# One-core attention stack: half of the first batch's query and key projections moved behind the first attention, its first stack loaded during it

## The chip, the cores and the metric

The kernel runs on 1 core of one Trainium2 chip. The metric is the device time of one launch in microseconds (us), as the median of several runs; lower is better. TensorE's matmul side is called PE, VectorE DVE, ScalarE ACT, GpSimd POOL, SyncE SP. SP issues nearly all DMAs.

## The reference

Two batches of 1024 tokens, width 256, 16 heads of 16, all in float32:

```
x  = x + attention(x Wq, ctx Wk, ctx Wv)      # a0: 77 context rows as keys
n  = layernorm(x)                             # norm 1
x  = x + attention(n Wq', n Wk', n Wv') Wo'   # a1: 1024 keys per batch
n  = layernorm(x)
x  = x + attention(n Wcq, ctx Wck, ctx Wcv) Wco   # a2: 77 keys again
x  = x + gelu(layernorm(x) W1) W2
```

## The kernel before

**Names.** Tokens stand in four blocks (tb 0 to 3) of 512; blocks 0 and 1 are the first batch. The attentions are A0, A1 and A2. Heads go in groups of four: 8 groups (g), and for each two halves of 512 queries, so 16 "q" per attention. An attention is a loop of steps t: 16 for A0 and A2 (one per q), 128 for A1 (eight tiles of 128 keys per q). A step makes four score matmuls (L815), whose exponentials ACT takes (L949), and the value products of the step before (L831).

**Row maxima.** A softmax row needs its maximum first. A "max" unit is a score matmul into the banks SM (PE L763 for A0 and A2, L758 for A1) and a reduction of it by DVE (L1065, L1062). A1's unit is 1.2 us of DVE; 26 of them ("lead") and one "rows" entry run ahead of A1's first step, the others two per step. "rows" turns a q's maxima into rows (PE L774 or L771, DVE copy L1075 or L1074 into mrow) that SP sends into the queries' tile (L636, L632); the scores of q wait for it. In A0 the rows of q + 2 are made in step q; in A1 those of q + 1 in key tile 4 of q.

**Stacks.** A group's queries and keys stand in a stack in SBUF. They get there by way of DRAM: a projection (L700, one chunk is half of the width for one block: 2 matmuls of 512 columns, 4 in the trace's count) is split into two parts, by ACT (L888) and DVE (L990); SP stores them to q_rows or k_rows (L554, two DMAs of 256 KB per chunk), and the function `stack` loads a group: for A1 10 DMAs (L584, L591), 1.5 MB, after SP itself has waited until the chunks that it reads have landed. Chunk i = 0 of the first batch feeds groups 0 and 1, chunk i = 1 groups 2 and 3. A1 has three stack buffers; buffer 0 and the keys' half of buffer 1 are free during A0. Padding rows of the buffers are set by POOL (`pad`, L1187); a stack load waits until they are.

**The order.** Nothing schedules itself: each engine walks the same lists and does its own part of each entry, strictly in order. UNDER_A0, UNDER_A1 and UNDER_A2 say what is put into which step; BEFORE_A1 is the list between A0 and A1. ("side", A1, a, b) is entries a to b of A1's 27 units ahead ("max" 0 to 19, "rows" 0, "max" 20 to 25). "x1" adds A0's result to a block and takes its statistics (DVE L1039, L1027, L1030; POOL takes the root), "norm" scales it (L1047), "t_ln1" transposes it (L704; ACT L920 or DVE L1002 write it to fm), "vals_s" is the value projection (L710, read by DVE L1007). "proj_kc" is the key projection of A2's context (two chunks of 154 columns), needed only by A2. A PE, DVE or SP entry that waits holds all that stands behind it on that engine.

**When stacks are loaded in A1.** The method `stacks_at` gives the step: 16 (g - 2) for group g, unless a projection that stands in UNDER_A1 in the first half pushes it back:

```
            for w in self.products(k):
                for g in range(QUAD + 2 * w[2], QUAD + 2 * w[2] + 2) if w[0][:5] == "proj_" else []:
                    at[g] = max(at[g], k + self.lag[1])
```

Of the kernel before, what the change touches and what calls it, by code (L numbers as in the profile page):

```python
# [35 lines left out]
KC = DIM // P  # L36
NT = TOK // P
BLK = 512
NB = TOK // BLK
TPB = BLK // P  # L40
QUAD = 4
# [6 lines left out]
SROWS = len(BANDS) * HD  # L48
# [22 lines left out]
def block_of(stage, tb, first=0, count=None):  # L71
    return [(stage, tb, i) for i in range(first, first + (count or PER[stage]))]


def chunks(i, *stages, tb):

    return [(stage, tb, i) for stage in stages]


def one_in_two(first, work):  # L80
# [5 lines left out]


UNDER_A0 = {
    **{n: [("load", n), ("pads", "a1", n)] for n in range(NB)},
    8: [("load", 4), ("load", 5)],  # L90
    9: [("x1", 0)],
    10: [("norm", 0, 0), ("x1", 1), ("load", 6), ("load", 7)],
    11: [("norm", 0, 1)] + block_of("t_ln1", 0),
    12: block_of("proj_q1", 0) + block_of("t_ln1", 1),
    13: block_of("proj_k1", 0),
    14: block_of("proj_q1", 1),
    15: block_of("proj_k1", 1),
}
UNDER_A1 = {
    **one_in_two(67, block_of("t_a1", 0) + block_of("out_1", 0) + [("stats", 1, 0)]  # L100
                 + block_of("t_a1", 1) + [("norm", 1, 0)] + block_of("out_1", 1) + [("stats", 1, 1)]
                 + block_of("t_ln2", 0) + [("norm", 1, 1)] + chunks(0, "proj_q2", tb=0) + block_of("t_ln2", 1)
                 + chunks(0, "proj_q2", tb=1) + chunks(1, "proj_q2", tb=0) + chunks(1, "proj_q2", tb=1)),
    98: [("pads", "a2", 0), ("keys", "a2")],
    112: [("pads", "a2", 1)],
    114: [("values", "a2", 0)],
# [30 lines left out]
class Attention:  # L137
# [61 lines left out]
    def chores(self, t):  # L199
# [3 lines left out]
A0 = Attention(0, 1, CTX, lead=12, rows_ahead=2, rows_at=0, buffers=4, banks=4, under=UNDER_A0,  # L203
               split_by=("pool", "dve"), lag=(0, 1))
A1 = Attention(1, SEQ // P, P, lead=26, rows_ahead=1, rows_at=4, buffers=3, banks=2, under=UNDER_A1,
               split_by=("pool", "pool"), lag=(1, 2))
# [11 lines left out]
BEFORE_A0 = [("proj_k0", 0), ("proj_q0", 0), ("keys", "a0"), ("proj_q0", 1), ("stack", "a0", 0), ("vals_c", 0),  # L218
             ("values", "a0", 0), ("stack", "a0", 1), ("proj_q0", 2), ("stack", "a0", 2), ("proj_q0", 3),
             ("side", A0, 0, len(A0.before)), ("stack", "a0", 3)]  # L220
BEFORE_A1 = [("stack", "a1", 0), ("vals_s", 0), ("x1", 2), ("vals_s", 1), ("x1", 3),
             ("norm", 0, 2), ("side", A1, 0, 2), ("t_ln1", 2),
             ("norm", 0, 3), ("side", A1, 2, 4), ("t_ln1", 3), ("pads", "a1", NB)]
SPREAD = [(stage, tb, i, 1) for stage, tb in (("proj_q1", 2), ("proj_k1", 2), ("proj_q1", 3), ("proj_k1", 3))
          for i in range(KC)]
BEFORE_A1 += [w for i, chunk in enumerate(SPREAD) for w in (("side", A1, 2 * i + 4, 2 * i + 6), chunk)]
BEFORE_A1 += [("values", "a1", 0), ("proj_kc", 0), ("side", A1, 2 * len(SPREAD) + 4, len(A1.before)), ("stack", "a1", 1),
              ("vals_s", 2), ("vals_s", 3), ("stack", "a1", 2)]
BEFORE_A2 = []
AFTER_A2 = [("t_a2", 2), ("t_a2", 3), ("up", 0), ("out_2", 2), ("out_2", 3), ("norm", 2, 2), ("norm", 2, 3),  # L230
# [1 line left out]
            ("down", 2), ("down", 3)]  # L232
PLAN = [(BEFORE_A0, A0), (BEFORE_A1, A1), (BEFORE_A2, A2), (AFTER_A2, None)]

# [13 lines left out]
def xattn_kernel(nc, xT_d, x_d, cT_d, ident_d, cols_d, rows_d, wq0, wk0, wv0, sa_w, so_w,  # L248
# [8 lines left out]
    with ctx:  # L257
# [21 lines left out]
        Kst = [stacks[:, n, 0] for n in range(A1.buffers)]  # L279
        Qst = [stacks[:, n, 1] for n in range(A1.buffers)]  # L280
# [108 lines left out]
        st_done = sem("st_done")  # L389
# [778 lines left out]
        def _(pool):  # L1168
# [4 lines left out]
            def step(ins):  # L1173

                ins.then_inc(pool_step, 1)
                steps[0] += 1
                pool.wait_ge(pool_step, steps[0])

            def space():

                used[0] += 1
                return gp.memset(spacer[:, used[0]:used[0] + 1], 0.0)


            def pad(tile, first, value):

                step(gp.memset(tile[first:first + 32].bitcast(FP32), value))  # L1187

            def padded():

                step(space())
                space().then_inc(pad_ready, 1)
                step(space())
# [8 lines left out]
            step(gp.memset(prob[64:P, :, :, :], 0.0))  # L1202
            step(gp.memset(nexp[:, :], -0.5))
            padded()

            def stationary(att, g):

# [24 lines left out]
            def pads(att, part):  # L1232

                step(space())
                if att is A1:
                    if part < 2:
                        pad(Kst[part], 32, 1.0)
                        pad(Kst[part], SROWS, 1.0)
                    elif part == 2:
                        pad(Qst[0], 32, 0.0)  # L1240
                        pad(Qst[0], SROWS, 0.0)
                        padded()
                    elif part == NB:
                        pool.wait_ge(st_done, A0.steps * QUAD)
                        pad(Qst[1], 32, 0.0)
                        pad(Qst[2], 32, 0.0)
                        pad(Kst[2], 32, 1.0)
                        pad(Kst[2], SROWS, 1.0)
                        padded()
                    step(space())  # L1250
                    return
                pool.wait_ge(st_done, (att.t0 - (2 - part) * HALVES * A1.kt) * QUAD)
                if part == 0:
                    pad(Kst[2], SROWS, TWO_ONES)
                    pad(Qst[2], SROWS, 0.0)
                elif part == 1:
                    pad(Qst[0], SROWS, 0.0)
                    pad(Kst[0], SROWS, 0.0)
                else:
                    pad(Qst[1], SROWS, 0.0)  # L1260
                padded()
# [145 lines left out]
```

## Time and profile before

| what | us |
|---|---|
| median of 3 runs (803.64 to 807.79) | 805.66 |
| the profiled execution's own time | 805.98 |
| its span in the trace | 804.2 |
| PE busy | 727.4 (90%) |
| DVE busy | 533.0 (66%) |
| ACT busy | 441.2 (55%) |
| POOL busy | 154.4 (19%) |
| chain that ended last: PE, DVE, DMA | 58%, 21%, 10% |

Times below are counted from the start of the span. A0's steps run from 48.85 to about 131, the list BEFORE_A1 from there to 200.86, A1 from 200.86.

### The profile page before, as it was taken

The numbers are of one execution on the slowest core, as the hardware profiler recorded it, in microseconds if no ns is written. First come the engines' busy times: TensorE is split into PE (matmuls) and PEld (weight loads), VectorE is DVE, ScalarE is ACT, GpSimd is POOL, SyncE is SP. The second block draws the span as 40 slices with busy tenths as digits, with TensorE's granted clock in tenths as the row PEclk, the third lists the DMA queues.
The fourth block names the chain that finished last, engine by engine and source line by source line (L and its number), as shares of the span: only waits on it lengthen the run. The fifth ranks groups of instructions, "written<-read, shape, count | busy, mean of one in ns | idle before, by whom it ended". The sixth has DMA issues, their size and how long they took to land.

```text
span 804.2 us, 13587 instructions
## 1 busy us (share of the span) xinstructions
PE 727.4 (90%) x5200; PEld 358.1 (45%) x5200; DVE 533.0 (66%) x851; ACT 441.2 (55%) x802; POOL 154.4 (19%) x341
## 2 busy tenths in 40 slices
PE   7568899488999999999999999997988997999998
PEld 3334445335333333333433433333454564556767
DVE  3436864697999999999899898852477774230001
ACT  4435544121888888887677677665635644323120
POOL 7335240431000000000001013150143223030000
PEclk9869899699999999999999999998999999999999
DMA  7977714536705050505013010016355600000001
GB/s 264 180 173 144 160 46 175 72 124 156 104 2 82 2 82 3 82 2 81 2 26 59 1 26 2 21 46 94 61 137 125 107 3 1 1 7 20 26 14 39
DMA packets 39087, 55.35 MB, mean 69 GB/s; under 512 B 8944, under 2 KB 24048, under 8 KB 39024
## 3 DMA queue, kind: packets, MB, share of 16 engines
q1 hardware_dynamic: 38736, 54.42, 32.3%
q8 instruction: 41, 0.67, 0.4%
q14 instruction: 22, 0.18, 0.1%
q10 hardware_dynamic: 288, 0.08, 0.1%
HBM read 36.31 MB, written 17.25 MB: 67 GB/s over the span
## 4 chain that ended last, share of the span: by engine, by line
PE 58%; DVE 21%; DMA 10%; ACT 3%; SPq 3%; issue 3%; POOL 1%; DVEq 0%; POOLq 0%; ACTq 0%
DVE nm L1062 15%; PE PV L831 14%; PE ST L815 11%; PE ST L723 5%; PE ST L719 5%; PE SM L758 5%; PE SM L710 3%; DMA V<-mrow 3%; DMA stacks<-mrow 3%; PE SM L700 3%; PE PV L723 2%; PE PV L719 2%; PE SM L704 2%; PE SM L763 2%; PE ST L710 2%
## 5 line engine op out<-in xcount | busy, mean ns | idle before, releaser
L949 ACT ACTIVATE prob<-ST 128x512 f32<-128x512 f32 (+1 forms) x640 | 349.6, 596 | 168.0 <-PE ST L815 158.9
L1062 DVE TENSOR_REDUCE nm<-SM 128x2 f32<-128x1024 f32 x256 | 308.8, 1221 | 16.1 <-PE SM L758 14.5
L831 PE MATMUL PV<-prob,Vst 128*32 128x256 f32 (+1 forms) x2304 | 202.9, 425 | 5.4 <-ACT pvT L938 2.8
L815 PE MATMUL ST<-stacks 64*128 64x512 f32 (+1 forms) x608 | 171.2, 483 | 6.5 <-DMA stacks<-mrow 4.1
L758 PE MATMUL SM<-stacks 64*128 64x512 f32 x512 | 109.5, 424 | 19.2 <-DMA stacks<-k_rows 10.2
L815 PEld LDWEIGHTS ST<-stacks 64*128 64x128 f32 (+1 forms) x608 | 61.8, 173 | 140.9 <-ACT prob L949 102.5
L1065 DVE TENSOR_REDUCE nm<-SM 128x4 f32<-128x308 f32 x128 | 58.0, 472 | 52.5 <-PE SM L763 50.8
L831 PEld LDWEIGHTS PV<-prob,Vst 128*32 128x32 f32 x2304 | 46.3, 109 | 95.4 <-issue 68.1
L758 PEld LDWEIGHTS SM<-stacks 64*128 64x128 f32 x512 | 49.5, 188 | 40.9 <-DVE nm L1062 22.8
L1017 DVE TENSOR_TENSOR X<-ST,X 128x256 f32<-128x256 f32 x18 | 7.5, 422 | 90.5 <-PE ST L723 73.7
L938 ACT ACTIVATE pvT<-PV 128x512 f32<-128x512 f32 x48 | 28.7, 599 | 33.7 <-PE PV L831 33.6
L719 PE MATMUL ST<-fm,V 128*128 128x512 f32 x96 | 42.6, 593 | 0.3 <-ACT fm L920 0.3
L1277 POOL CAST mp<-na 128x16 fp32r<-128x16 f32 x16 | 3.2, 198 | 199.8 <-DVE na L1097 199.8
L1303 POOL TENSOR_TENSOR X<-X,bc 128x256 f32<-128x256 f32 x48 | 34.2, 743 | 26.7 <-DVE A L1047 26.7
L763 PE MATMUL SM<-stacks 96*128 96x77 bf16 x384 | 30.9, 208 | 6.9 <-DMA stacks<-q_parts 4.1
L763 PEld LDWEIGHTS SM<-stacks 96*128 96x128 bf16 x384 | 26.6, 106 | 23.1 <-issue 9.0
L780 PE MATMUL SM<-ident,pvT 128*128 128x128 f32 x192 | 31.0, 285 | 2.8 <-ACT pvT L938 1.2
L1187 POOL MEMSET stacks<- 32x2048 f32 x18 | 32.4, 1800 | 1.0
L700 PE MATMUL SM<-fm,early 128*128 128x512 f32 x64 | 31.0, 607 | 0.0
L719 PEld LDWEIGHTS ST<-fm,V 128*128 128x128 f32 x96 | 18.1, 190 | 21.7 <-issue 20.8
L700 PE MATMUL ST<-fm,early 128*128 128x512 f32 x48 | 25.1, 654 | 1.9 <-DMA fm<-in_xT 1.0
L927 ACT ACTIVATE early<-ST,cols 128x512 f32<-128x512 f32 x12 | 8.3, 688 | 33.1 <-PE ST L719 33.1
(114 smaller groups left out, 718.3 us busy)
## 6 DMA issues: line engine op xcount, KB each, us to landing
stacks<-q_parts SPq DMA_DIRECT2D x72, 128.0 KB, 4.9
q_parts<-split SPq DMA_DIRECT2D x16, 384.0 KB
q_rows<-parts SPq DMA_DIRECT2D x16, 256.0 KB
k_rows<-parts SPq DMA_DIRECT2D x16, 256.0 KB
stacks<-q_rows SPq DMA_DIRECT2D x16, 256.0 KB
stacks<-k_rows SPq DMA_DIRECT2D x16, 256.0 KB
V<-q_parts SPq DMA_DIRECT2D x24, 128.0 KB, 5.3
fm<-in_xT SPq DMA_DIRECT2D x4, 512.0 KB, 7.5
```

The costliest lines, as they stand in the source:

```text
L700: last = mm(ps[:, 0:width], weight[:, k, w0 + i * P:w0 + (i + 1) * P], src[:, k, c0:c0 + width], start=(k == 0), stop=(k == KC - 1))
L710: last = mm(ps[:, 0:DIM], fm[:, k, t0:t0 + P], weight[:, k, w0:w0 + DIM], start=(k == 0), stop=(k == KC - 1))
L719: last = mm(ps[:, 0:BLK], w_1[:, k, i * P:(i + 1) * P], fm[:, k, tb * BLK:(tb + 1) * BLK], start=(k == 0), stop=(k == KC - 1))
L723: last = mm(ps[:, 0:DIM], hid[tb % 2][:, f, i * P:(i + 1) * P], w_2[:, f, :], start=(f == 0), stop=(f == FF // P - 1))
L758: last = mm(ps[:, s * BLK:(s + 1) * BLK], Q[rows, n, c0:c0 + P], Kst[g % att.buffers][rows, n, c * BLK:(c + 1) * BLK], start=True, stop=True)
L763: last = mm(ps[:, h * CTX:(h + 1) * CTX], Q[0:SROWS, h, c0:c0 + P], keys_of(att, g, h, 0)[0:SROWS], start=True, stop=True)
L815: mm(ST[0:att.keys, n % 3, :], keys_of(att, g, h, kt), QST[att.name][g % att.buffers][rows, at, j * BLK:(j + 1) * BLK], start=True, stop=T ...
L831: last = mm(PV[h * 32:(h + 1) * 32, queries], Vst[:, g % 2, kt, h, :], prob[:, t % 2, h, queries], start=(kt == 0 and first == 0), stop=(k ...
L949: act_fn(prob[0:att.keys, t % 2, h, :], ST[0:att.keys, n % 3, :], ACT.Exp, scale=SCALE if att.whole else 1.0).then_inc(exp_done, 1)
L1062: ins = vec.tensor_reduce(nm2[:, q % 2, c, tile, 2 * n:2 * n + 2], ps.rearrange("p (s k) -> p s k", s=2), AX.X, ALU.max, negate=True)
L1065: ins = vec.tensor_reduce(nm[:, q % 2, v, :], ps[:, 0:QUAD * CTX].rearrange("p (h k) -> p h k", h=QUAD), AX.X, ALU.max, negate=True)
L1303: ins = gp.tensor_tensor(X[:, t, :], X[:, t, :], bc[:, (B_SO, B_CO, B_F2)[n], :], ALU.add)
```

## The change

In UNDER_A0 the four chunks i = 1 of proj_q1 and proj_k1 of blocks 0 and 1 leave steps 12 to 15; the four chunks i = 0 stand in steps 12 and 13, and the load of stack 0 stands in step 13. The moved chunks stand in BEFORE_A1. There the load of stack 1 comes first, after the one round of padding that is left; the two first max units stand ahead of both "x1"; and proj_kc has gone to steps 40 and 42 of A1. The padding of buffer 0 and of the keys of buffer 1 moves from A0's first steps to POOL's start.

```diff
--- before.py
+++ after.py
@@ -86,21 +86,20 @@
 
 
 UNDER_A0 = {
-    **{n: [("load", n), ("pads", "a1", n)] for n in range(NB)},
+    **{n: [("load", n)] for n in range(NB)},
     8: [("load", 4), ("load", 5)],
     9: [("x1", 0)],
     10: [("norm", 0, 0), ("x1", 1), ("load", 6), ("load", 7)],
     11: [("norm", 0, 1)] + block_of("t_ln1", 0),
-    12: block_of("proj_q1", 0) + block_of("t_ln1", 1),
-    13: block_of("proj_k1", 0),
-    14: block_of("proj_q1", 1),
-    15: block_of("proj_k1", 1),
+    12: chunks(0, "proj_q1", "proj_k1", tb=0) + block_of("t_ln1", 1),
+    13: chunks(0, "proj_q1", "proj_k1", tb=1) + [("stack", "a1", 0)],
 }
 UNDER_A1 = {
     **one_in_two(67, block_of("t_a1", 0) + block_of("out_1", 0) + [("stats", 1, 0)]
                  + block_of("t_a1", 1) + [("norm", 1, 0)] + block_of("out_1", 1) + [("stats", 1, 1)]
                  + block_of("t_ln2", 0) + [("norm", 1, 1)] + chunks(0, "proj_q2", tb=0) + block_of("t_ln2", 1)
                  + chunks(0, "proj_q2", tb=1) + chunks(1, "proj_q2", tb=0) + chunks(1, "proj_q2", tb=1)),
+    **{40 + 2 * i: [("proj_kc", 0, i)] for i in range(KC)},
     98: [("pads", "a2", 0), ("keys", "a2")],
     112: [("pads", "a2", 1)],
     114: [("values", "a2", 0)],
@@ -218,13 +217,13 @@
 BEFORE_A0 = [("proj_k0", 0), ("proj_q0", 0), ("keys", "a0"), ("proj_q0", 1), ("stack", "a0", 0), ("vals_c", 0),
              ("values", "a0", 0), ("stack", "a0", 1), ("proj_q0", 2), ("stack", "a0", 2), ("proj_q0", 3),
              ("side", A0, 0, len(A0.before)), ("stack", "a0", 3)]
-BEFORE_A1 = [("stack", "a1", 0), ("vals_s", 0), ("x1", 2), ("vals_s", 1), ("x1", 3),
-             ("norm", 0, 2), ("side", A1, 0, 2), ("t_ln1", 2),
-             ("norm", 0, 3), ("side", A1, 2, 4), ("t_ln1", 3), ("pads", "a1", NB)]
+BEFORE_A1 = [("pads", "a1", 0), ("stack", "a1", 1), ("proj_q1", 0, 1, 1), ("proj_k1", 0, 1, 1), ("vals_s", 0),
+             ("side", A1, 0, 2), ("x1", 2), ("proj_q1", 1, 1, 1), ("proj_k1", 1, 1, 1), ("vals_s", 1), ("x1", 3),
+             ("norm", 0, 2), ("side", A1, 2, 4), ("t_ln1", 2), ("norm", 0, 3), ("side", A1, 4, 6), ("t_ln1", 3)]
 SPREAD = [(stage, tb, i, 1) for stage, tb in (("proj_q1", 2), ("proj_k1", 2), ("proj_q1", 3), ("proj_k1", 3))
           for i in range(KC)]
-BEFORE_A1 += [w for i, chunk in enumerate(SPREAD) for w in (("side", A1, 2 * i + 4, 2 * i + 6), chunk)]
-BEFORE_A1 += [("values", "a1", 0), ("proj_kc", 0), ("side", A1, 2 * len(SPREAD) + 4, len(A1.before)), ("stack", "a1", 1),
+BEFORE_A1 += [w for i, chunk in enumerate(SPREAD) for w in (("side", A1, 2 * i + 6, 2 * i + 8), chunk)]
+BEFORE_A1 += [("values", "a1", 0), ("side", A1, 2 * len(SPREAD) + 6, len(A1.before)),
               ("vals_s", 2), ("vals_s", 3), ("stack", "a1", 2)]
 BEFORE_A2 = []
 AFTER_A2 = [("t_a2", 2), ("t_a2", 3), ("up", 0), ("out_2", 2), ("out_2", 3), ("norm", 2, 2), ("norm", 2, 3),
@@ -1202,6 +1201,10 @@
             step(gp.memset(prob[64:P, :, :, :], 0.0))
             step(gp.memset(nexp[:, :], -0.5))
             padded()
+            for tile, value in ((Kst[0], 1.0), (Qst[0], 0.0), (Kst[1], 1.0)):
+                pad(tile, 32, value)
+                pad(tile, SROWS, value)
+            padded()
 
             def stationary(att, g):
 
@@ -1233,21 +1236,12 @@
 
                 step(space())
                 if att is A1:
-                    if part < 2:
-                        pad(Kst[part], 32, 1.0)
-                        pad(Kst[part], SROWS, 1.0)
-                    elif part == 2:
-                        pad(Qst[0], 32, 0.0)
-                        pad(Qst[0], SROWS, 0.0)
-                        padded()
-                    elif part == NB:
-                        pool.wait_ge(st_done, A0.steps * QUAD)
-                        pad(Qst[1], 32, 0.0)
-                        pad(Qst[2], 32, 0.0)
-                        pad(Kst[2], 32, 1.0)
-                        pad(Kst[2], SROWS, 1.0)
-                        padded()
-                    step(space())
+                    pool.wait_ge(st_done, A0.steps * QUAD)
+                    pad(Qst[1], 32, 0.0)
+                    pad(Qst[2], 32, 0.0)
+                    pad(Kst[2], 32, 1.0)
+                    pad(Kst[2], SROWS, 1.0)
+                    padded()
                     return
                 pool.wait_ge(st_done, (att.t0 - (2 - part) * HALVES * A1.kt) * QUAD)
                 if part == 0:
```

PE between A0's last transposes (L780, L779 in the changed kernel; all lines below 101 stand one lower there) and the first projection of block 2. Before:

```order
L780 MATMUL SM<-ident,pvT 128x128 x8
L710 MATMUL ST<-early,fm 128x256 x2
L710 MATMUL PV<-early,fm 128x256 x2
L710 MATMUL ST<-early,fm 128x256 x6
L710 MATMUL PV<-early,fm 128x256 x2
L710 MATMUL ST<-early,fm 128x256 x4
L758 MATMUL SM<-stacks 128x512 x4
L704 MATMUL ST<-ident,A 128x128 x4
L704 MATMUL PV<-ident,A 128x128 x4
L758 MATMUL SM<-stacks 128x512 x4
L704 MATMUL ST<-ident,A 128x128 x8
L758 MATMUL SM<-stacks 128x512 x4
```

After the change:

```order
L779 MATMUL SM<-ident,pvT 128x128 x8
L699 MATMUL ST<-fm,early 128x512 x2
L699 MATMUL PV<-fm,early 128x512 x2
L709 MATMUL ST<-early,fm 128x256 x6
L709 MATMUL PV<-early,fm 128x256 x2
L757 MATMUL SM<-stacks 128x512 x4
L699 MATMUL ST<-fm,early 128x512 x4
L709 MATMUL ST<-early,fm 128x256 x2
L709 MATMUL PV<-early,fm 128x256 x2
L709 MATMUL ST<-early,fm 128x256 x4
L757 MATMUL SM<-stacks 128x512 x4
L703 MATMUL ST<-ident,A 128x128 x4
```

The two moved chunks of block 0 stand where the second half of the value projections stood, the first two max units (SM<-stacks) stand behind four value projections, and two more chunks and four value projections stand behind them.

DVE from the first "x1" of that list to the max units (TENSOR_REDUCE). Before:

```order
L1039 TENSOR_TENSOR X<-X,A 128x256 x4
L1027 BN_STATS stats<-X 128x6 x4
L1030 BN_AGGR mv<-stats 128x2 x4
L1007 TENSOR_TENSOR V<-ST,bc 128x4x64
L1007 TENSOR_TENSOR V<-PV,bc 128x4x64
L1007 TENSOR_TENSOR V<-ST,bc 128x4x64 x2
L1039 TENSOR_TENSOR X<-X,A 128x256 x4
L1027 BN_STATS stats<-X 128x6 x4
L1030 BN_AGGR mv<-stats 128x2 x4
L1047 TENSOR_SCALAR A<-X,mv,rstd 128x256 x4
L1062 TENSOR_REDUCE nm<-SM 128x2 x2
L1047 TENSOR_SCALAR A<-X,mv,rstd 128x256 x4
```

After the change:

```order
L1061 TENSOR_REDUCE nm<-SM 128x2 x2
L1038 TENSOR_TENSOR X<-X,A 128x256 x4
L1026 BN_STATS stats<-X 128x6 x4
L1029 BN_AGGR mv<-stats 128x2 x4
L989 SCALAR_TENSOR_TENSOR parts<-ST,cols,parts 128x512 x2
L1006 TENSOR_TENSOR V<-ST,bc 128x4x64
L1006 TENSOR_TENSOR V<-PV,bc 128x4x64
L1006 TENSOR_TENSOR V<-ST,bc 128x4x64 x2
L1038 TENSOR_TENSOR X<-X,A 128x256 x4
L1026 BN_STATS stats<-X 128x6 x4
L1029 BN_AGGR mv<-stats 128x2 x4
L1046 TENSOR_SCALAR A<-X,mv,rstd 128x256 x4
```

Both "x1" (X<-X,A and the two rows behind it) and the first "norm" (A<-X,mv,rstd) stood ahead of the first max units and now stand behind them, with two readings of moved chunks (parts<-ST).

SP in A1, around the load of stack 4 (zeros, q_rows, k_rows; c_parts is proj_kc's store, mrow the rows). Before:

```order
L632 DMA stacks<-mrow 2x4x128 x8
L584 DMA stacks<-zeros 2x16x128
L591 DMA stacks<-q_rows 32x2x1024
L591 DMA stacks<-q_rows 16x2x1024
L591 DMA stacks<-k_rows 32x2x1024
L591 DMA stacks<-k_rows 16x2x1024
L584 DMA stacks<-zeros 2x16x128
L591 DMA stacks<-q_rows 32x2x1024
L591 DMA stacks<-q_rows 16x2x1024
L591 DMA stacks<-k_rows 32x2x1024
L591 DMA stacks<-k_rows 16x2x1024
L632 DMA stacks<-mrow 2x4x128 x8
```

After the change:

```order
L562 DMA c_parts<-split 128x3x154
L583 DMA stacks<-zeros 2x16x128
L590 DMA stacks<-q_rows 32x2x1024
L590 DMA stacks<-q_rows 16x2x1024
L590 DMA stacks<-k_rows 32x2x1024
L590 DMA stacks<-k_rows 16x2x1024
L583 DMA stacks<-zeros 2x16x128
L590 DMA stacks<-q_rows 32x2x1024
L590 DMA stacks<-q_rows 16x2x1024
L590 DMA stacks<-k_rows 32x2x1024
L590 DMA stacks<-k_rows 16x2x1024
L631 DMA stacks<-mrow 2x4x128 x4
```

The load of stack 4 stood at step 32, two sets of rows (8 DMAs) ahead of it and the rows of q = 5 and 6 behind it; now it stands at step 42, behind proj_kc's first store and right ahead of the rows of q = 6.

## Rows read from the trace of the kernel before

**Rows 1.** The chain that ended last, 125 to 156: start us, us, what

```profile
131.79 6.36 DMA k_rows<-parts
...
143.03 9.30 DMA stacks<-k_rows
...
152.47 0.81 PE SM L758 x2
```

**Rows 2.** Timeline of PE: start, us, line, operation, in brackets idle before and its releaser

```profile
113.59 1.88 PE L700 MATMUL SM<-fm,early 128*128 128x512 f32 x4
...
152.47 1.22 PE L758 MATMUL SM<-stacks 64*128 64x512 f32 x4 [10.17 <-DMA stacks<-k_rows]
...
200.86 0.50 PE L815 MATMUL ST<-stacks 64*128 64x512 f32 x2 [0.78 <-DVE V L1007]
```

**Rows 3.** Timeline of SP's queue: first store of step 12, stack 0, stack 4

```profile
113.49 3.37 SPq L554 DMA_DIRECT2D q_rows<-parts  x4
...
138.17 0.73 SPq L584 DMA_DIRECT2D stacks<-zeros  x1
...
283.91 0.64 SPq L584 DMA_DIRECT2D stacks<-zeros  x1
```

**Rows 4.** Windows: from:to, length, PE clock, DMA share, GB/s

```profile
116.00:121.50 5.50, 1.00 0.50 172
...
285.40:295.40 10.00, 1.00 1.01 159
```

**Rows 5.** Timeline of DVE

```profile
114.36 0.80 DVE L1002 TENSOR_SCALAR fm<-SM,cols 128x512 f32<-128x512 f32 x1
...
120.42 0.40 DVE L1075 COPY mrow<-SM 12x512 bf16<-12x512 bf16 x1
...
139.22 1.42 DVE L1039 TENSOR_TENSOR X<-X,A 128x256 f32<-128x256 f32 x4
...
142.16 0.39 DVE L1007 TENSOR_TENSOR V<-ST,bc 128x256 f32<-128x256 f32 x1
...
146.39 1.34 DVE L1047 TENSOR_SCALAR A<-X,mv,rstd 128x256 f32<-128x256 f32 x4
153.37 2.36 DVE L1062 TENSOR_REDUCE nm<-SM 128x2 f32<-128x1024 f32 x2 [5.64 <-PE SM L758]
...
159.87 2.36 DVE L1062 TENSOR_REDUCE nm<-SM 128x2 f32<-128x1024 f32 x2 [0.59 <-PE SM L758]
...
186.14 6.86 DVE L1062 TENSOR_REDUCE nm<-SM 128x2 f32<-128x1024 f32 x6
```

**Rows 6.** Timeline of POOL: A0's start, and the padding ahead of A1

```profile
23.50 0.24 POOL L1229 COPY Vst<-Vc 77x64 f32<-77x64 f32 x1 [6.73 <-DVE Vc L1012]
30.21 2.39 POOL L1310 TENSOR_TENSOR parts<-parts,split 128x512 f32<-128x512 f32 x2 [6.47 <-ACT split L882]
...
159.97 7.36 POOL L1187 MEMSET stacks<- 32x2048 f32 x4
```

**Rows 7.** Timeline of PE in A0's steps 3 and 5

```profile
64.53 0.38 PE L774 MATMUL SM<-identb,mp 128*12 128x128 bf16 x4 [1.71 <-POOL mp L1289]
...
71.87 0.41 PE L815 MATMUL ST<-stacks 128*77 128x512 bf16 x1 [0.62 <-DMA stacks<-mrow]
```

**Rows 8.** The chain that ended last, the row DMA of A0's step 3

```profile
65.45 6.37 DMA stacks<-mrow
```

**Rows 9.** Windows: PE, PEld, DVE, ACT, POOL busy (instructions), PE clock, DMA share, GB/s

```profile
152.40:160.00 7.60, 7.11 (x28) 4.79 (x28) 6.04 (x9) 3.11 (x4) 2.85 (x6) 0.50 0.00 0
```

**Rows 10.** Timeline of PE: proj_kc's second chunk, then A1's steps 42, 44 and 48

```profile
184.81 0.69 PE L700 MATMUL PV<-ctxT,early 128*128 128x154 f32 x4
...
311.63 0.50 PE L815 MATMUL ST<-stacks 64*128 64x512 f32 x2
...
318.25 0.28 PE L771 MATMUL SM<-ident,mp 128*32 128x128 f32 x1
...
327.06 0.50 PE L815 MATMUL ST<-stacks 64*128 64x512 f32 x2
```

## The prediction

> **What bounds the kernel now.** I read the chain of waits in order of time first, since the change touches one place, the passage from A0 to A1. There the chain leaves the engines: a store of a key part takes 6.36 us, then SP issues stack 0, whose last DMA takes 9.30 us, and PE starts the first max unit at 152.47 [rows 1]. The timeline of PE shows the price: 10.17 us idle [rows 2]. That is what the change is after. But the stretch behind it, up to A1's first step at 200.86, must be read as well, and there the timeline of DVE decides: two max units and one reading of a chunk follow each other almost without a gap from 159.87 until the last six units end at 193.00 (186.14 + 6.86) [rows 5]. So behind the stack DVE is the bound. And what does DVE do while PE waits for the stack? It adds x1 of two blocks and scales one (139.22 to 147.73) [rows 5]. PE's idle time is not the kernel's idle time.
>
> **When stack 0 arrives after the change.** (a) A0's start. POOL's six memsets of 1.84 us (7.36 / 4) [rows 6], 11.0 us, move from A0's first steps to POOL's start. There POOL is idle 6.73 and 6.47 us, 13.2 in all, around a 0.24 us copy that nothing wants before A0's steps [rows 6]: hidden; without that cover they would push the split of block 3's queries back. What they free is 1.71 us of PE in step 3 [rows 7]. Little of it survives: step 5 waits for its row until 71.87 [rows 7], a small DMA issued at 65.45 that takes 6.37 us [rows 8], because the six loads of a stack stand in front of it. Only the issue of those moves up, by about half a microsecond. I take 0.8 us; the bounds are 0 and 3.4 (twice the 1.71, since the step behind the stall is slowed as well).
>
> (b) Step 13's first chunk is now of block 1, whose fm is written by DVE until 115.16 (114.36 + 0.80) [rows 5], where the old one started at 113.59 [rows 2]: +1.6 us. The row copy of that step, before at 120.42 to 120.82 [rows 5], ends at 120.8 + 1.6 - 0.8 = 121.6. SP issues the row in 0.8 us and then the stores of both chunks, from 122.4.
>
> (c) Four stores took from 113.49 [rows 3] to 121.5, where their data ends [rows 4]: 8.0 us. So they land at 130.6 with 0.2 for the notice, where SP got on at 138.17 before [rows 3] with 14 of 16 stores done: six fewer.
>
> (d) Ten DMAs of a stack took from 283.91 [rows 3] to 295.4 [rows 4] when nothing was in their way: 11.5 us. Before it was 14.3 (138.17 to 152.47), with chunk stores still moving. I take 11.5 and 0.3 for the start: **the first max unit at 142.4 instead of 152.47, 10.1 us earlier** (bounds 141 and 145). PE, relieved of two chunks on balance, waits there still, some 4 us.
>
> **What stands behind it.** Call D the start of DVE's first max unit, 0.9 us after PE's: 153.37 before [rows 5], 143.3 after. Before, the last unit ended at D + 39.6. After the change DVE has, in its order: two units 2.3 (to D + 2.3); x1 of block 2, 2.9 (139.22 to 142.16 [rows 5]), D + 5.2; two readings of moved chunks 0.7 each, D + 6.5; four readings of values, the last held by PE, D + 7.9; x1 of block 3, D + 10.8; norm 1.3, D + 12.2; two units, D + 14.5; norm, D + 15.8; two units, D + 18.1; then the row of chunks, which began at D + 6.5 (159.87) before and kept 33.1 us. It has one unit fewer behind its chunks (the two that stand earlier, less the one that the last chunk's row entry displaces): 31.8. The last unit ends at D + 50.1. So **10.5 us of work moved from under the wait to behind it**: two x1 5.9, one norm 1.3, two chunk readings 1.4, value readings 1.4, the rest order. The 10.1 us are eaten by it. From the last unit to A1's first step it stays 7.9 us (193.0 to 200.86).
>
> **PE's clock.** After the wait of 10 us PE ran at 0.50 of its clock, which is 1.2 GHz, for 7.60 us, with 7.11 us busy, and DVE only 6.04 [rows 9]. Before there was little for PE to do there. Now two chunks of 1.9 us and four value projections of 0.9 stand there, 7.3 us at full speed, which is about what DVE takes (7.9). If the clock is at half for the first 4 us, PE is 2 us late, and with it both x1. I take 2.0 less 0.4 for the transposes, which now run at full clock: +1.6 (bounds 0 and 5). The Trainium skill (TensorE: Matmul & The Clock Gate, "What's actually happening") states that the throttled state is the default and sustained activity releases it. By that rule the new wait of 4 us, too, may cost the clock; if it doesn't, the sum is that of the rival "clock kept".
>
> **proj_kc and stack 4.** In BEFORE_A1 the two chunks were covered by DVE. In A1's steps PE and DVE are both full. A chunk of four 154-column matmuls keeps PE 0.55 to 0.69 us [rows 10], with 0.3 us of DVE; I take 1.2 us for both (bounds 0.5 and 2). And stack 4 goes from step 32 to step 42. Its use as keys and queries is late enough (the first max unit of group 4 is in step 51). But the rows of q = 6 are queued right behind it on SP. Step 42 starts at 311.63 [rows 10]; with ACT's and POOL's parts of proj_kc and the store, SP starts the stack near 316.6 (the step's 2.5 us, 0.6 for the first chunk, and some 1.9 for ACT, POOL and the store), and by the 11.5 us above its data ends at 328.1. The row DMAs, ready at about 319, behind step 44's transposition at 318.25 [rows 10], come in behind that data as in rows 8, at 328.5. Step 48 wants them at 327.06 [rows 10] + 1.2 = 328.3. I take +0.4 (bounds 0 and 3). Next late, if that fails, is nothing: stack 5 loads at step 48 as before.
>
> **Sum.** -10.1 + 10.5 + 1.6 + 1.2 + 0.4 = +3.6 us on the profiled execution's 805.98, so 809.6; that execution stands 0.3 above the median 805.66, so **809.3** as a median. POOL's second round of padding (7.4 us from A0's last score) and the load of stack 1 lie beside waits; the chunk stores queued behind stack 1 land by about 160 (142.1 + 11.5 + the 8.0 of four stores, less the overlap), and the chunks of block 2 want those buffers from D + 21.6, 165, on; past that point each us late would cost one.
>
> **The rivals.** *Padding stalls fully given back* (not slower): if step 5's row is not held by the loads, A0 gains 3.4 instead of 0.8 and the stack chain with it: 809.3 - 2.6 = 806.7. For it: the 1.71 us are real PE idle time. Against: rows 8. It decides from an A0 gain of about 3 us on; one of 4.4 would make the change's sum zero.
> *Clock kept*: 809.3 - 2.0 = 807.3. For it: the wait is 4 us instead of 10.
> *Work hides after all*: DVE had 1.6 us free of 7.60 in rows 9. If the moved work uses these, 1.6 less: 807.7. Against: the order is fixed, and the gaps are waits for PE at its half clock.
> *Stacks in each other's way* (slower): stack 1 is issued from 136 on, while stack 0's data moves until 142. If the engines share out their time, stack 0 lands up to 4 us later: 813.3. Against: in rows 8 a later DMA waits behind the earlier ones. The Trainium skill (DMA: Bandwidth & Descriptors, "Queues, rings and completion order") says the same, that each engine takes its ring's descriptors in order; by it this rival costs nothing and 809.3 stands.
>
> **How the numbers follow.** Forecast 0.45, own range 807 to 812; padding 0.15; clock 0.13; work hides 0.07; stacks 0.12; gains together 0.08 (all three 803.1). About 0.5%, 4.0 us, is what a measurement of this kernel can tell from no change. Slower by more starts at 809.7: nearly half of the forecast and the rival of the stacks, and large clock or row costs, 0.42. Faster by more (under 801.6) needs all three gains and an overrated term besides: 0.07. Between: 0.51. Range 802.5 to 814: it takes in all single rivals and leaves out a sum below them.
>
> **What would show it.** In the changed kernel's trace: PE's wait for k_rows ends near 142.4 and is 3 to 6 us long; SP starts stack 0 near 130.6; DVE's first "x1" of block 2 stands behind two max units; A1's first step is at 202 to 204 instead of 200.86; PE's clock is at half for some 4 us behind the wait; a wait of PE for mrow at step 48 of under 2 us; A1's steps 40 to 43 are 0.6 us longer each for a chunk. The prediction is wrong if A0's step 5 starts more than 2 us earlier, or if the time between the first max unit and A1's first step is not near 60 us (48.4 before).

## The result and the profile after

The changed kernel takes **821.37 us** (median of 4 runs, 817.22 to 823.72), the kernel before 806.01 beside it (median of 4, 803.64 to 807.79): a ratio of 1.019, 95% interval 1.0155 to 1.0224. It is slower, by four times what was forecast. The profiled execution took 820.4 us, with a span of 818.6, which is 14.4 more than before.

I divided both spans, and later those of all experiments, at the same four events: A0's first step, SP's issue of stack 0, PE's first max unit (the stack has landed), A1's first step.

| us | A0's first step | to issue of stack 0 | to first max unit | to A1's first step | to the end | span |
|---|---|---|---|---|---|---|
| before | 48.85 | 89.3 | 14.3 | 48.4 | 603.3 | 804.2 |
| after | 50.10 | 82.5 | 14.6 | 61.3 | 610.1 | 818.6 |
| difference | +1.3 | -6.8 | +0.3 | +12.9 | +6.8 | +14.4 |

A0's first step lay between 46.1 and 50.1 in the kernels of this study. Kernels that are alike up to there differ in it by up to 4.0 us (50.1 in the changed kernel, 46.1 in x1_first below), so the first column can't be put down to the change.

The chain that ended last, in order of time, answers to [rows 1]:

```profile
126.20 6.38 DMA k_rows<-parts
...
137.45 9.59 DMA stacks<-k_rows
...
147.18 1.22 PE SM L757 x4
```

PE's timeline at the same places as [rows 2], with the first wait behind the stack, and step 48 of A1:

```profile
116.02 1.96 PE L699 MATMUL SM<-fm,early 128*128 128x512 f32 x4 [1.55 <-DVE fm L1001]
...
147.18 1.22 PE L757 MATMUL SM<-stacks 64*128 64x512 f32 x4 [8.82 <-DMA stacks<-k_rows]
148.33 4.82 PE L699 MATMUL ST<-fm,early 128*128 128x512 f32 x8
...
161.41 1.08 PE L703 MATMUL ST<-ident,A 128*128 128x128 f32 x4 [4.15 <-DVE A L1046]
...
208.49 0.50 PE L814 MATMUL ST<-stacks 64*128 64x512 f32 x2 [0.78 <-DVE V L1006]
...
341.87 0.79 PE L814 MATMUL ST<-stacks 64*128 64x512 f32 x2 [5.33 <-DMA stacks<-mrow]
```

Three things stand there. The wait for the stack is hardly shorter (8.82 us instead of 10.17), though it ends 5.3 us earlier. A new wait of 4.15 us follows, for a norm that was done long before in the old order. And there is a wait of 5.33 us for a q's rows at step 48, where there was none [rows 10]. SP's timeline gives the issues that belong to them (compare [rows 3]):

```profile
124.15 1.21 SPq L553 DMA_DIRECT2D q_rows<-parts  x2
...
132.63 0.73 SPq L583 DMA_DIRECT2D stacks<-zeros  x1
...
138.00 0.65 SPq L583 DMA_DIRECT2D stacks<-zeros  x1
...
326.22 0.67 SPq L583 DMA_DIRECT2D stacks<-zeros  x1
...
331.38 2.62 SPq L631 DMA_DIRECT2D stacks<-mrow  x4
```

And DVE's timeline behind the stack, beside [rows 5]:

```profile
148.08 2.36 DVE L1061 TENSOR_REDUCE nm<-SM 128x2 f32<-128x1024 f32 x2 [9.26 <-PE SM L757]
150.35 1.42 DVE L1038 TENSOR_TENSOR X<-X,A 128x256 f32<-128x256 f32 x4
...
156.98 1.42 DVE L1038 TENSOR_TENSOR X<-X,A 128x256 f32<-128x256 f32 x4
...
159.91 1.35 DVE L1046 TENSOR_SCALAR A<-X,mv,rstd 128x256 f32<-128x256 f32 x4
...
195.06 5.74 DVE L1061 TENSOR_REDUCE nm<-SM 128x2 f32<-128x1024 f32 x5
```

DVE is idle for 9.26 us and then does both x1 and the norm, which it did under the wait before. Windows sum it up. Their columns are the window, its length, busy us of PE, PEld (PE's weight loads), DVE, ACT and POOL (instructions), PE's clock as a share of 2.4 GHz, the DMA share and GB/s. First the stretch from the first max unit to A1's first step in the kernel before:

```profile
152.47:200.86 48.39, 42.10 (x142) 22.41 (x143) 40.38 (x48) 10.45 (x18) 13.75 (x21) 0.88 0.44 116
```

The same in the changed kernel, then pieces of it and two windows behind the wait at step 48:

```profile
147.18:208.49 61.31, 49.69 (x158) 26.30 (x159) 50.79 (x82) 9.99 (x14) 9.84 (x16) 0.86 0.57 141
143.00:150.00 7.00, 2.82 (x6) 1.37 (x7) 1.92 (x2) 0.00 (x0) 0.00 (x0) 0.50 1.07 139
...
161.00:169.00 8.00, 6.71 (x25) 4.78 (x26) 7.41 (x10) 3.12 (x4) 6.22 (x9) 0.50 0.34 133
...
198.50:201.00 2.50, 2.41 (x6) 1.71 (x7) 2.30 (x3) 0.00 (x0) 0.00 (x0) 0.50 0.65 168
...
342.00:344.00 2.00, 2.00 (x12) 0.56 (x12) 0.87 (x1) 1.08 (x2) 0.00 (x0) 0.50 1.07 122
344.00:346.00 2.00, 2.00 (x18) 0.91 (x16) 1.06 (x2) 1.14 (x3) 0.09 (x1) 0.71 1.06 170
```

DVE has 10.4 us more work in this stretch (50.79 less 40.38), PE 7.6 more. PE's clock is at half, 1.2 GHz, in four places, each behind a time in which PE had waited or had little to do.

### The profile page after: what moved, and what is told of

Read it like the earlier page. It is cut to its first block, busy times and chain, and to the rows that moved or that the text cites. A ratio compares the mean times of both kernels' runs of the same rounds, so it can differ in the third digit from the quotient of the medians.

```text
span 818.6 us, 13576 instructions
## 1 busy us (share of the span) xinstructions
PE 729.7 (89%) x5200; PEld 358.6 (44%) x5200; DVE 533.4 (65%) x853; ACT 440.5 (54%) x800; POOL 154.0 (19%) x332
## 4 chain that ended last, share of the span: by engine, by line
PE 60%; DVE 21%; DMA 10%; SPq 3%; ACT 3%; issue 3%; POOL 1%; DVEq 0%; POOLq 0%; ACTq 0%
PE PV L830 14%; DVE nm L1061 13%; PE ST L814 11%; PE ST L722 5%; PE ST L718 5%; PE SM L757 5%; PE SM L709 3%; PE SM L699 2%; DMA stacks<-mrow 2%; PE ST L699 2%; DMA V<-mrow 2%; PE ST L709 2%; PE SM L762 2%; PE SM L703 2%; PE PV L722 2%
## 5 line engine op out<-in xcount | busy, mean ns | idle before, releaser
L699 PE MATMUL ST<-fm,early 128*128 128x512 f32 x60 | 32.9, 684 | 2.2 <-DMA fm<-in_xT 1.3
L1186 POOL MEMSET stacks<- 32x2048 f32 x18 | 32.4, 1799 | 10.4 <-PE ST L814 9.5
L779 PE MATMUL SM<-ident,pvT 128*128 128x128 f32 x192 | 30.5, 281 | 2.8 <-ACT pvT L937 1.2
L1277 POOL CAST mp<-nm 128x16 bf16<-128x16 f32 x32 | 6.3, 197 | 110.9 <-DVE nm L1064 110.8
L703 PE MATMUL SM<-ident,A 128*128 128x128 f32 x112 | 20.0, 309 | 7.0 <-DVE A L1046 6.1
```

Source lines behind the costliest of these rows:

```text
L699: last = mm(ps[:, 0:width], weight[:, k, w0 + i * P:w0 + (i + 1) * P], src[:, k, c0:c0 + width], start=(k == 0), stop=(k == KC - 1))
L703: last = nc.tensor.transpose(ps[:, n * P:(n + 1) * P], A[:, tb * TPB + n, i * P:(i + 1) * P], ident[:, :])
```

## The experiments

Two losses had to be told apart: the passage behind the stack (+12.9) and A1 (+6.8). For each I had a theory, and in the passage two rivals: that the stacks delay each other, and that PE's clock, not DVE's order, is the price. Parts of the span are read from one traced execution of each kernel; medians are of all its runs. `...` in a code cut stands for code left out.

### The A1 side: proj_kc, and what it does to stack 4

The first kernel, kc_back, is the changed one with proj_kc back in the list ahead of A1:

```diff
-    **{40 + 2 * i: [("proj_kc", 0, i)] for i in range(KC)},
-BEFORE_A1 += [("values", "a1", 0), ("side", ...
+BEFORE_A1 += [("values", "a1", 0), ("proj_kc", 0), ("side", ...
```

> The changed kernel with the two chunks of proj_kc put back into the list ahead of A1, so that stack 4 is loaded at step 32 again. Theory (late stack): PE's wait of 5.3 us for the rows at step 48 comes from stack 4's load standing right ahead of those rows; it goes, and with it the two chunks' own 1.3 us and half a microsecond of half clock: 814.5 instead of 821.4, and no wait of PE for mrow over 1 us in A1 between steps 40 and 50. Rival (passage only): the whole loss is made ahead of A1's first step and the wait is one that another place would show instead: 820 to 821.

Measured: 811.10 us (10 runs, 807.18 to 815.86), ratio to before 1.0076, 1.0041 to 1.0111. That is 3.4 us less than the theory said. The part from A1's first step to the end is 603.5 us, as before (603.3), and there is no wait for rows at step 48. The traced execution also had PE's clock at 0.94 in the passage, the highest of all kernels here.

The second, kc_no_push, leaves proj_kc in A1, but it no longer pushes stack 4 back:

```diff
-    ... if w[0][:5] == "proj_" else []:
+    ... if w[0][:5] == "proj_" and w[0] != "proj_kc" else []:
```

> The changed kernel with proj_kc still in A1's steps 40 and 42, but the rule that pushes a stack's load behind a projection doesn't count it, so stack 4 loads at step 32. Theory (late stack): the 5.3 us wait goes, the chunks' own cost stays: 815.5, about 1.3 above the kernel with proj_kc put back. Rival (the chunks themselves, in steps where PE and DVE are full, with their readings on ACT and POOL): 819 to 821, since the load's place alone does nothing.

Measured: 813.52 us (4 runs, 811.96 to 815.59), ratio 1.0114, 1.0064 to 1.0163. The part from A1's first step on is 603.1 us: the two chunks in A1's steps cost nothing that can be seen there. The medians can't exclude the 1.2 us that were forecast for them: this one is 2.4 us above that of kc_back, and the intervals of the two ratios overlap. In SP's timeline of this kernel stack 4 leaves at 291.84, and the rows of q = 6 have no load right ahead of them:

```profile
291.84 0.65 SPq L583 DMA_DIRECT2D stacks<-zeros  x1
...
328.59 2.60 SPq L631 DMA_DIRECT2D stacks<-mrow  x4
```

The third, kc_alone, is the kernel before with only this part of the change, the push with it:

```diff
+    **{40 + 2 * i: [("proj_kc", 0, i)] for i in range(KC)},
-BEFORE_A1 += [("values", "a1", 0), ("proj_kc", 0), ("side", ...
+BEFORE_A1 += [("values", "a1", 0), ("side", ...
```

> The kernel before with one part of the change alone: proj_kc in A1's steps 40 and 42, with the load of stack 4 pushed to step 42. Theory (late stack): a wait for the rows of about 5 us at step 48 appears here as well, 1.3 us for the chunks: 806.0 + 6.8 = 812.8. Rival (the wait needs what the rest of the change does to A1): 807.3.

Measured: 813.25 us (4 runs, 810.27 to 814.77), ratio 1.0104, 1.0053 to 1.0155. PE's timeline shows the same wait at step 48:

```profile
333.36 0.80 PE L816 MATMUL ST<-stacks 64*128 64x512 f32 x2 [6.24 <-DMA stacks<-mrow]
```

So the push is the cause, not the chunks: with it the wait is there, without it the wait is gone. A1's part is 6.8 us longer in the changed kernel and 6.0 in kc_alone. Of the 6.8, 5.33 are the wait; behind it PE ran at half its clock for some 3.2 us (all of 342 to 344, and 58% of the next window, whose clock is 0.71), which is 1.6 us. By the medians the push is 7.9 us (821.37 less 813.52), and the push with the chunks 7.0 (813.25 less 806.26, the kernel before beside kc_alone).

### The padding alone

The kernel before with only the padding moved to POOL's start (shown are the lines added and the first that goes; the old padding code goes as in the change):

```diff
-    **{n: [("load", n), ("pads", "a1", n)] for n in range(NB)},
+    **{n: [("load", n)] for n in range(NB)},
+            for tile, value in ((Kst[0], 1.0), (Qst[0], 0.0), (Kst[1], 1.0)):
+                pad(tile, 32, value)
+                pad(tile, SROWS, value)
+            padded()
```

> The kernel before with the padding of buffer 0 and of the keys of buffer 1 at POOL's start, nothing else. Theory (A0 held by its row DMAs, as predicted): step 5 waits longer for its row instead of step 3 for POOL, 0 to 1 us faster, 805 to 806. Rival (padding stalls given back): 802.6. Rival (POOL's memsets at the start slow what runs beside them): A0's first step later by about 1.2 us as in the changed kernel, 807.

Measured: 804.96 us (10 runs), ratio 1.0005, 0.9977 to 1.0034. From A0's first step to the issue of stack 0 it takes 89.3 us, exactly as before. PE's wait of 1.71 us in step 3 is gone, and the wait for the row DMA of step 5 is longer, 3.61 us instead of 0.62:

```profile
66.97 0.62 PE L815 MATMUL ST<-stacks 128*77 128x512 bf16 x1 [3.61 <-DMA stacks<-mrow]
```

But that wait doesn't take all: step 5's row releases PE 20.8 us behind A0's first step (66.97 less 46.21), against 23.0 before (71.87 less 48.85). These 2.3 us are lost in the steps behind it. Step 9's first score is 0.6 us ahead (83.75 less 46.21, against 86.98 less 48.85), and the value products at 106.25 stand where those at 108.85 stood, 60.0 us behind A0's first step. What takes them there was not isolated: the chain of before passes through a further row DMA (90.87), that of pads_alone through x1 and the norm on DVE. The rival "padding stalls fully given back" is gone.

### The passage: do the stacks delay each other?

This kernel, stack1_late, is kc_back with stack 1 issued behind the moved chunks' stores, so that stack 0 has the queue for itself:

```diff
-BEFORE_A1 = [("pads", "a1", 0), ("stack", "a1", 1), ("proj_q1", 0, 1, 1), ...
+BEFORE_A1 = [("pads", "a1", 0), ("proj_q1", 0, 1, 1), ...
-             ... ("proj_k1", 1, 1, 1), ("vals_s", 1), ("x1", 3),
+             ... ("proj_k1", 1, 1, 1), ("stack", "a1", 1), ("vals_s", 1), ("x1", 3),
```

> Stands on the kernel with proj_kc put back (811.1). One edit: stack 1 is issued behind the stores of all moved chunks instead of right behind stack 0. Theory (stacks in each other's way): stack 0 takes 11.5 us from its first issue instead of 14.4, PE's first max unit comes 2.9 us earlier, and so does A1's first step: 808.2. Rival (a stack takes 14 to 15 us at this place whatever stands behind it, as it did in the kernel before and in all runs so far): 811.

Measured: 813.33 us (9 runs, 806.32 to 815.84), ratio 1.0100, 1.0069 to 1.0130. Stack 0 takes 13.6 us from issue to first max unit, against 14.4 in kc_back. The 0.8 us lie within what stack 0 takes in all twelve kernels, the kernel before included (13.6 to 15.0), and the median did not fall. A stack takes about 14 us here, whether a second one stands behind it or not.

### The passage: the order of DVE's work

x1_first is kc_back with both x1 and the first norm ahead of the first two max units, but the moved chunks of block 1 still behind them:

```diff
-             ("side", A1, 0, 2), ("x1", 2), ("proj_q1", 1, 1, 1), ("proj_k1", 1, 1, 1), ("vals_s", 1), ("x1", 3),
-             ("norm", 0, 2), ("side", A1, 2, 4), ...
+             ("x1", 2), ("x1", 3), ("norm", 0, 2), ("side", A1, 0, 2), ("proj_q1", 1, 1, 1), ("proj_k1", 1, 1, 1),
+             ("vals_s", 1), ("side", A1, 2, 4), ...
```

> Stands on the kernel with proj_kc put back (811.1). One edit: both x1 and the first norm stand ahead of the first two max units in the list, so DVE does them while stack 0 is loaded. Theory (cover lost): 7.2 us of DVE work leaves the stretch behind the stack, PE's wait of 4.1 us for the norm goes, and from the first max unit to A1's first step it is 51 to 52 us instead of 58.4: 804. Rival (PE's half clock and its two moved chunks set the stretch): 809 to 811.

Measured: 809.24 us (10 runs, 805.06 to 814.60), ratio 1.0059, 1.0028 to 1.0089. DVE's busy time in the passage fell from 50.61 (kc_back) to 43.52 us, and the stretch did not follow: 58.0 us after 58.4 (by the medians it gained 1.9). The timelines of PE and DVE show why; the window of the stretch stands below them:

```profile
143.65 1.22 PE L756 MATMUL SM<-stacks 64*128 64x512 f32 x4 [8.90 <-DMA stacks<-k_rows]
144.80 5.44 PE L698 MATMUL ST<-fm,early 128*128 128x512 f32 x8
...
160.87 3.78 PE L698 MATMUL ST<-fm,early 128*128 128x512 f32 x4
```

```profile
149.35 0.75 DVE L988 SCALAR_TENSOR_TENSOR parts<-ST,cols,parts 128x512 fp32r<-128x512 f32 x1 [2.45 <-ACT parts L886]
...
165.47 0.75 DVE L988 SCALAR_TENSOR_TENSOR parts<-ST,cols,parts 128x512 fp32r<-128x512 f32 x1 [3.01 <-ACT parts L886]
```

```profile
143.65:201.65 58.00, 51.02 (x165) 26.51 (x166) 43.52 (x54) 11.68 (x20) 7.83 (x15) 0.87 0.59 150
```

PE is busy 51.02 us of 58.00. The chunks behind the max unit run at half clock (a pair takes 5.44 us, and a chunk at 160.87 3.78 instead of 1.98), and DVE, which reads them behind ACT, waits 2.45 and 3.01 us for them. So my theory, that DVE's order alone makes the stretch long, falls: with that work gone, PE with its own moved work, partly at half clock, is the bound. How much of the missing gain is the moved work and how much the clock was not isolated: the mean clock was 0.87 here and 0.94 in kc_back, an estimate of 4 us of PE's time (13% of 58.0 less 6% of 58.4). Both edits together, combo:

> Both edits together on the kernel with proj_kc put back: x1 and norm ahead of the first max units, stack 1 behind the moved chunks' stores. Theory (cover lost, and stacks in each other's way): 801 to 802, faster than the kernel before (806.3). Rival (a stack's time doesn't depend on the one behind it): 804.

Measured: 808.96 us (6 runs), ratio 1.0035, 1.0002 to 1.0067; stretch 57.8 us. Both the theory (801 to 802) and its rival (804) were too low, since both took x1_first's gain for given. The edits don't add to anything that can be seen over x1_first alone.

The counter-test, x1_late, is the kernel before with only the first two max units drawn ahead of both x1 and the first norm. They come to stand ahead of block 1's value projections (`vals_s` 1) too:

```diff
-BEFORE_A1 = [("stack", "a1", 0), ("vals_s", 0), ("x1", 2), ("vals_s", 1), ("x1", 3),
-             ("norm", 0, 2), ("side", A1, 0, 2), ("t_ln1", 2),
+BEFORE_A1 = [("stack", "a1", 0), ("vals_s", 0), ("side", A1, 0, 2), ("x1", 2), ("vals_s", 1), ("x1", 3),
+             ("norm", 0, 2), ("t_ln1", 2),
```

> The kernel before with one edit: its first two max units stand ahead of both x1 and the first norm, so that this DVE work no longer lies under PE's wait for stack 0. Theory (cover lost): first max unit at the same time, A1's first step later by the 7.2 us of that work less the gaps that DVE has behind it: 811 to 813. Rival (the moved chunks are what costs, not this work): 806 to 807.

Measured: 814.76 us (4 runs, 813.92 to 819.36), ratio 1.0138, 1.0099 to 1.0177: about 10 us, more than expected. PE's timeline:

```profile
149.70 1.22 PE L758 MATMUL SM<-stacks 64*128 64x512 f32 x4 [12.76 <-DMA stacks<-k_rows]
...
161.54 1.09 PE L704 MATMUL ST<-ident,A 128*128 128x128 f32 x4 [5.09 <-DVE A L1047]
```

With no projection moved out of A0, the stretch grows from 48.4 to 58.7 us, as in kc_back, and the wait for the norm is there. Taking the cover from under the wait is by itself enough for what the whole change does to the passage. The cover taken away is not DVE's alone, though: four value projections of PE, with their four readings on DVE, left it along with both x1 and the norm, which the expectation had overlooked, and PE's wait for the stack is 12.76 us instead of 10.17. DVE's share and PE's are not told apart by this kernel.

### Filling the wait with everything that there is

If both engines' moved work is the price, both must go back under the wait. fill_wait is kc_back once more, with all four moved chunks, both blocks' values, both x1 and the first norm ahead of the first max unit:

```diff
-BEFORE_A1 = [..., ("proj_k1", 0, 1, 1), ("vals_s", 0),
-             ("side", A1, 0, 2), ("x1", 2), ("proj_q1", 1, 1, 1), ("proj_k1", 1, 1, 1), ("vals_s", 1), ("x1", 3),
-             ("norm", 0, 2), ("side", A1, 2, 4), ...
+BEFORE_A1 = [..., ("proj_k1", 0, 1, 1), ("proj_q1", 1, 1, 1), ("proj_k1", 1, 1, 1), ("vals_s", 0),
+             ("x1", 2), ("vals_s", 1), ("x1", 3),
+             ("norm", 0, 2), ("side", A1, 0, 2), ("side", A1, 2, 4), ...
```

> The change with proj_kc back in BEFORE_A1, and with everything that PE and DVE can do while stack 0 is on its way put ahead of the first two max units: the four moved chunks, the value projections of blocks 0 and 1, both x1 and the first norm. PE then has some 13 us of work from 129 on, DVE some 12. Theory (the stretch grew because the work that had covered the wait stood behind it, and the rest was PE at half its clock after an idle wait): PE's wait for k_rows falls from 8.6 to 9.4 us to under 2.5, the clock stays at full behind it, and the time from the first max unit to A1's first step falls from 58 to 48 to 51 us; A1 starts near 194 to 197 with A0's start at 48, and the time is 797 to 803 us, under before. Rival (the moved work keeps the same length wherever it stands, since PE or DVE are full over the whole passage and the stack's arrival doesn't decide): the first max unit is late by the work that stands ahead of it, the sum of both is as in x1_first, and the time is 807 to 811.

Measured: **801.43 us** (8 runs, 799.71 to 804.46), before 805.73 beside it (19 runs): ratio 0.9949, 0.9927 to 0.9971. It is faster than before, and 20 us faster than the change. PE's wait:

```profile
146.25 1.22 PE L756 MATMUL SM<-stacks 64*128 64x512 f32 x4 [2.50 <-DMA stacks<-k_rows]
```

DVE's first reduction:

```profile
149.10 4.61 DVE L1060 TENSOR_REDUCE nm<-SM 128x2 f32<-128x1024 f32 x4
```

The windows ahead of the max unit and behind it:

```profile
131.00:146.25 15.25, 12.75 (x48) 8.39 (x46) 10.01 (x29) 2.75 (x4) 4.19 (x7) 0.98 0.92 136
...
146.25:198.74 52.49, 42.81 (x141) 22.67 (x142) 43.22 (x61) 10.39 (x18) 10.29 (x18) 0.84 0.67 172
...
146.00:151.00 5.00, 1.85 (x6) 0.82 (x6) 5.00 (x15) 0.00 (x0) 2.91 (x5) 0.50 1.02 143
```

The stack lands when it did in kc_back, but now PE was busy for 12.75 and DVE for 10.01 of the 15.25 us ahead of it, and PE has in the stretch what it had before the change (42.81 us, 42.10 before). One part of the expectation failed: the clock was to stay at full, yet it is at 0.50 from 146 to 156, behind a wait of only 2.50 us.

This half clock is not what makes the stretch 52.5 us instead of 48 to 51, for from 146 to 156 DVE is busy without a gap and PE only 6.51 us of the 10. Two other things can be read. When the stack landed DVE still had statistics and the norm to do, and its first reduction starts 2.85 us behind PE's first max unit (149.10 less 146.25), where it was 0.90 before (153.37 less 152.47): 2.0 us. And at the end of the stretch, where PE with the values of blocks 2 and 3 is the bound, the clock is at half for 6.8 us (of 187 to 194) against 3.4 (of 191 to 195) in the kernel before: an estimate of 1.7 us. Together that is 3.7 of the 4.1 us by which the stretch exceeds that of before.

The Trainium skill (TensorE: Matmul & The Clock Gate, "What's actually happening") states that the throttled state is the default and sustained activity releases it; the trace agrees, with 0.50 behind the wait of 2.50 us and full clock again from about 156, when PE had worked for 6.51 of 10 us.

fill_wait2 is the same with the moved chunks of block 1 behind the first x1:

> As fill_wait, with the moved chunks of block 1 behind the first x1 and the values of block 0 instead of ahead of them, so that PE's and DVE's shares alternate. Theory: the same as fill_wait within 2 us (797 to 804), since both fit under the stack's 14 us. Rival: whichever order leaves DVE or PE waiting for the other at the start of the passage shows it as a later first max unit, by more than 2 us.

Measured: 801.67 us (12 runs, 798.40 to 805.72), ratio 0.9957, 0.9931 to 0.9982; stretch 51.9 us. No difference.

| us | to issue of stack 0 | to first max unit | to A1's first step | to the end | median |
|---|---|---|---|---|---|
| pads_alone | 89.3 | 14.0 | 49.8 | 603.3 | 804.96 |
| kc_alone | 89.5 | 14.7 | 48.7 | 609.3 | 813.25 |
| kc_no_push | 84.2 | 14.8 | 63.0 | 603.1 | 813.52 |
| kc_back | 82.7 | 14.4 | 58.4 | 603.5 | 811.10 |
| stack1_late | 83.5 | 13.6 | 59.2 | 602.8 | 813.33 |
| x1_first | 83.0 | 14.6 | 58.0 | 604.3 | 809.24 |
| combo | 82.7 | 13.8 | 57.8 | 607.8 | 808.96 |
| x1_late | 88.8 | 13.8 | 58.7 | 603.7 | 814.76 |
| fill_wait | 82.1 | 15.0 | 52.5 | 600.3 | 801.43 |
| fill_wait2 | 83.2 | 14.1 | 51.9 | 606.5 | 801.67 |

Each row is one execution. The last part of the span lies between 600.3 and 607.8 in the ten kernels without the late stack, the kernel before among them, though nothing in A1 and A2 but kc_no_push's two chunks differs between them. The executions traced of combo and fill_wait2 were the slowest of their kernels. A difference of a few us in that column is therefore no finding; the medians, and the waits in the timelines, carry the verdicts.

## Why the prediction was wrong in size

The direction was right, though a slowdown beyond the noise was given only 0.42. The size was not: 809.3 forecast, 821.4 measured, outside the range. The traced span grew by 14.4 us where 3.6 were forecast. Of the 10.8 us between them 5.2 lie in A1 (+6.8 against 1.2 and 0.4), 2.8 in the time that stack 0 takes (+0.3 against -2.5), 0.8 in the stretch (+12.9 against 10.5 and 1.6), 0.8 in the padding, and 1.3 in A0's start, which is scatter (each rounded). Step by step:

- **(a) Padding**, 0.8 us: nothing came (pads_alone). The lower bound was the truth, but not for the reason given: step 5 did start 2.3 us earlier in pads_alone, counted from A0's first step, and the steps behind it lost that again. POOL's start hid the memsets as said.
- **(b) Step 13**, +1.6: right, the wait for fm is 1.55 us.
- **(c) Four stores**, 8.0 us: right, 8.5 from 124.15 to 132.63. The issue of stack 0 came 6.8 us earlier, counted from A0's first step; forecast were 7.6, the 0.8 of the padding being the difference.
- **(d) Ten DMAs of a stack**, 11.5 us and 0.3: this step failed. It took 14.55 us (132.63 to 147.18), so the first max unit came 6.5 us earlier, counted from A0's first step, and not 10.1. I had put the 14.3 us of before down to chunk stores in the way. They were not: stack1_late and the kernels with six stores fewer lie between 13.6 and 15.0 too. The fault is one of reading: I took the end of stack 4's data from the window in which the DMA share falls, and that is not when the waiting engine is released. In the kernel before, stack 0 read in the same way ends at 150.3, and PE starts at 152.47:

```profile
149.00:150.00 1.00, 0.00 (x0) 0.00 (x0) 0.00 (x0) 0.00 (x0) 1.00 (x3) 0.50 0.94 94
150.00:151.00 1.00, 0.00 (x0) 0.00 (x0) 0.00 (x0) 0.00 (x0) 0.71 (x2) 0.50 0.26 33
151.00:152.00 1.00, 0.00 (x0) 0.00 (x0) 0.00 (x0) 0.00 (x0) 0.00 (x0) 0.50 0.05 16
```

  That is 12.1 us by the share and 14.3 by the release. Why those 12.1 are 0.6 more than stack 4's 11.5 stays open.
- **Work moved from under the wait**, 10.5 us: right in size (the parts listed add to 49.9 and not 50.1, a slip of 0.2). DVE's busy time in the stretch rose by 10.4. But the reason was half, and that the number holds is in part luck: the price is fixed by DVE and PE together. x1_first took 7.1 us from DVE and the stretch shrank by 0.4, since PE's moved chunks and values, partly at half clock, then bound.
- **PE's clock**, +1.6: 2.4 us of the stretch's growth are left for it (12.9 less 10.5), within its bounds; that is a remainder and no measurement. PE was at half clock in three places of the stretch instead of one, and the last of them, 198.5 to 201, stands in the kernel before as well, near 191 to 195. In kc_back and kc_no_push, which differ in the stretch by two short chunks of proj_kc, it is 58.4 and 63.0 us, with a mean clock of 0.94 and 0.84: the clock goes with a difference of over 4 us, and what decides it in a given run was not isolated.
- **proj_kc**, +1.2: nothing to be seen in A1's part (kc_no_push, 603.1 against 603.3), but one execution of each and medians 2.4 us apart don't exclude it either.
- **Rows behind stack 4**, +0.4 (bounds 0 and 3): the second failed step, and the larger. The place, the queue and the step were named rightly. The wait was 5.33 us, and with the half clock behind it the price was 6.8 where 0.4 was forecast. Stack 4 left at 326.22, 2.0 us later than worked out once A1's later start is taken off, since POOL's second operation on the first chunk came two steps behind its first (325.15 and 320.24); and stack and rows took 15.6 us (to 341.82) where I had 11.9, the mis-read 11.5 once more. The last row DMA itself, in the chain:

```profile
333.38 8.44 DMA stacks<-mrow
```

  The bound of 3 us was drawn around the estimate, not from a row; the row that it should have come from is stack 0's own 14.3.

Of the rivals, *padding given back* is excluded by pads_alone, *clock kept* by four stretches at 0.50, *work hides* by DVE's 10.4 us. *Stacks in each other's way* is worth 0.8 us at most, not 4 (stack1_late): a load behind the first hardly delays it. The Trainium skill (DMA: Bandwidth & Descriptors, "Queues, rings and completion order") has it that each engine takes its ring's descriptors in order, and the trace agrees, with 13.6 against 14.4 us.

## What to carry to other kernels

Before a wait is shortened, list what runs under it on every engine, and keep that work ahead of the waiting instruction; the change lost by moving work behind the wait, and the same projections placed under it, with proj_kc back in its old place, made the kernel faster (801.4 against 805.7 us). Read a load's time from its issue to the release of the engine that waits for it, never to the point where the DMA share falls: here that was 14.3 against 12.1 us, and the error entered the sum twice. When a rule moves a large load to a later step, look at the small DMAs that are queued behind it and at the step that needs them: 1.5 MB ahead of four row DMAs cost 6.8 us.

## What the runs showed of the hardware

- In fill_wait PE worked for 12.75 us without a gap, waited 2.50 us and was then at half clock for 10 us (146 to 156), busy for 6.51 of them. Behind the wait of 4.15 us in the changed kernel the clock stayed at 0.50 for 8 us, with PE busy for 6.71 of them.
- Half clock need not show in the time: in fill_wait's 146 to 156 DVE was busy for all 10 us and set the pace. Where PE was the bound it showed: a chunk took 3.78 us instead of 1.98 in x1_first, and DVE waited 3.01 us.
- A stack of 1.5 MB took 13.6 to 15.0 us from issue to release in all kernels, whether 8 or 16 DMAs of chunk stores had gone ahead of it in A0's last steps and whether a second stack stood behind it.
- Removing a wait of 1.71 us of PE in A0's step 3 put step 5 2.3 us earlier and stack 0's issue not at all (89.3 us from A0's first step, with and without).
